# A two-layer gated cross-attention and expert kernel: another order of gathers, posts and sends, and idle products

## The reference

```
x = x + tanh(g_xattn[0]) * causal_attention(layernorm(x), ctx, ctx)       # 16 heads of 32
x = x + tanh(g_ffn[0])   * experts(layernorm(x))                          # 32 experts, 8 chosen per row
x = x + tanh(g_xattn[1]) * cross_attention(layernorm(x), ctx, weights)    # q, k, v projections, RMS norms, output projection
x = x + tanh(g_ffn[1])   * (layernorm(x) @ ternary(weight).T + bias)
```

## Time and profile before

| | |
|---|---|
| median of three runs | 1456.93 us |
| the profiled execution | 1449.55 us |
| its span, first to last instruction | 1447.8 us |
| TensorE busy | 1290.1 us (89%), mean granted clock 0.963 |
| VectorE, ScalarE, POOL busy | 940.0, 897.2, 519.5 us |
| gathers of rows (L709), 120 | 191.2 us of POOL |
| first layer | up to about 297 us |
| experts | about 297 to 922 us |
| second layer | from about 922 us |

### The profile page before, as it was taken

One profiled execution on the slowest core, in us unless ns is written; L12 is line 12 of the kernel. 1 busy time (PEld: TensorE's weight loads), 2 busy tenths in 40 slices (PEclk: granted clock), 3 DMA queues, 4 the chain that ended last, 5 costly groups with the idle time before them and its releaser, 6 DMA issues. The chain is left out here.

```text
span 1447.8 us, 39176 instructions
## 1 busy us (share of the span) xinstructions
PE 1290.1 (89%) x11501; PEld 836.5 (58%) x11502; DVE 940.0 (65%) x2347; ACT 897.2 (62%) x1845; POOL 519.5 (36%) x537
## 2 busy tenths in 40 slices
PE   3999999559999999999999999756899999999984
PEld 3777777425556656665556666333565656656652
DVE  4699897655566655656555633164777888888863
ACT  4777776325566666666566666425667777777661
POOL 2036564664335333321000000655544555552000
PEclk9999999779999999999999999978999999999997
DMA  3036445499888676766766544856646646653000
GB/s 104 31 130 224 181 171 184 173 311 324 290 309 282 235 234 226 244 213 215 233 229 210 193 146 145 167 89 88 102 69 108 106 71 117 103 72 75 16 8 23
DMA packets 96136, 233.49 MB, mean 161 GB/s; under 512 B 11808, under 2 KB 11808, under 8 KB 91424
## 3 DMA queue, kind: packets, MB, share of 16 engines
q0 software_dynamic: 33712, 113.79, 31.5%
q1 hardware_dynamic: 62320, 118.34, 24.6%
HBM read 140.84 MB, written 91.24 MB: 160 GB/s over the span
## 5 line engine op out<-in xcount | busy, mean ns | idle before, releaser
L1614 PE MATMUL bank<-wh,xT 128*128 x1280 | 340.1, 328 | 6.3 <-DVE hp L1729 5.4
L709 POOL DMA_INDIRECT xs<-y_tiles,slot_ix x120 | 191.2, 1593 | 219.9 <-DMA y_tiles<-ysb 99.9
L1614 PE MATMUL bank<-wl,xT 128*128 x640 | 209.4, 327 | 0.0
L1719 DVE SCALAR_TENSOR_TENSOR hv<-bank,sg 128x192 f32<-128x192 f32 x160 | 57.0, 356 | 220.1 <-ACT sg L1673 174.6
L1688 ACT ACTIVATE ysb<-bank,xg 128x512 f32<-128x512 f32 x160 | 110.0, 687 | 117.5 <-PE bank L1638 117.5
L1614 PEld LDWEIGHTS bank<-wh,xT 128*128 128x128 f16 x1280 | 125.6, 98 | 83.6 <-issue 13.4
L1667 ACT ACTIVATE xT<-bank 128x1024 f16<-128x1024 f16 x160 | 162.7, 1017 | 15.3 <-PE bank L1602 15.3
L1638 PE MATMUL bank<-wh,hT 128*128 x480 | 155.8, 379 | 0.8 <-issue 0.5
L1849 PE MATMUL bank<-w_hi,halfT 128*128 128x512 f16 x384 | 127.1, 393 | 23.5 <-DVE accb L1966 22.1
L334 ACT ACTIVATE l_probs<-bank,l_bias 128x256 f32<-128x256 f32 x256 | 118.9, 473 | 39.0 <-DVE l_bias L368 38.6
L1508 POOL DMA_DIRECT2D raw<-in_experts_dram x30 | 16.8, 560 | 333.2 <-DVE wl L1745 325.4
(11 more groups left out here) (282 smaller groups left out, 3060.4 us busy)
## 6 DMA issues: line engine op xcount, KB each, us to landing
xg<-x_slots SPq DMA_DIRECT2D x160, 272.0 KB, 2.8
y_tiles<-ysb SPq DMA_DIRECT2D x160, 256.0 KB, 2.7
raw<-in_experts_dram POOLq DMA_DIRECT2D x30, 1280.0 KB, 7.3
x_slots<-blank SPq DMA_DIRECT2D x33, 272.0 KB, 4.0
xs<-in_x_dram SPq DMA_DIRECT2D x8, 512.0 KB, 6.4
cbuf<-in_ctx_dram SPq DMA_DIRECT2D x8, 512.0 KB, 4.4
stage<-in_mats_dram POOLq DMA_DIRECT2D x4, 1024.0 KB, 6.4
room<-in_ctx_dram SPq DMA_DIRECT2D x8, 512.0 KB, 5.7
```

The costliest lines, as they stand in the source:

```text
L709: return nc.gpsimd.indirect_dma_start(to, None, self.y_tiles[0 : (MT + 1 - k) * P, :], ix, compute_op=ALU.add)
L1614: last = nc.tensor.matmul(bGU[t.place % 2][:, 0:GU], xT[:, t.place % 2, xo + c * P : xo + (c + 1) * P], wp[:, bass.ds(w, 1), c * GU : (c + ...
```

## The change

- Six instead of four of batch 0's gather turns are in the experts' block (`LAST_ADDS`).
- In the second layer's opening three of batch 1's gathers come before POOL's "P1"; on VectorE xc moves ahead of P2, and xn and sx ahead of P3; on ScalarE sx moves ahead of k0 and k1.
- A table `LAST1` replaces `SIDE1` in batch 7: batch 6's pieces come earlier, and the pieces with "=" are batch 7's own, with t = 0. The bank's order of use in that batch is `LAST_USES`.
- Ten of POOL's sends at the first layer's end lose their waits.
- TensorE gets products into bank 3 whose result nobody reads: 18 after the sum of the ternary weights, 2 after each of x0 and x1, 16 at the end of the block.

```diff
-LAST_ADDS = 4
+LAST_ADDS = 2
@@ BEGIN1
-    act=["sc", "T0", "T1", "P0", "P1", "k0", "k1", "sx", "T2", "T3", "P4", "P5", "k2", "k3"],
+    act=["sc", "T0", "T1", "P0", "P1", "sx", "k0", "k1", "T2", "T3", "P4", "P5", "k2", "k3"],
     pool=["P1", "xc", "P5"],
-    dve=["sc", "P0", "P1", "P2", "P3", "xc", "xn", "sx", "k0", "k1", "P4", ...
+    dve=["sc", "P0", "P1", "xc", "P2", "xn", "sx", "P3", "k0", "k1", "P4", ...
@@
+LAST1 = dict(
+    pe={0: ["a0"], 1: ["a1"], 2: ["<c0"], 3: ["c1"], 4: ["<d0"], 5: ["<d1"], 8: ["<g0", "g1"], 9: ["h0"], 10: ["h1"], 11: ["=a0"],
+        13: ["<=c0"], 14: ["=d0"]},
+    act={1: ["b0", "b1"], 2: ["c0"], 3: ["c1"], 7: ["f0", "f1"], 8: ["g0"], 9: ["g1"], 12: ["=b0"], 13: ["=c0"]},
+    pool={5: ["d1"]},
+    dve={0: ["a0", "a1"], 1: ["b0"], 2: ["<b1"], 4: ["d0"], 5: ["d1"], 6: ["e"], 7: ["f0", "f1"], 10: ["h0"], 11: ["h1"],
+         12: ["<=a0", "=b0"], 15: ["=d0"]})
@@ side1
-def side1(table, b, step, early, do_prep, do_post):
+def side1(eng, b, step, early, do_prep, do_post):
+    table = LAST1[eng] if b.n == B - 1 else SIDE1[eng]
...
+        if piece.startswith("="):
+            do_post(b, piece[1:])
@@ layer0, POOL
-            for n in (1, 2):
-                pool.wait_ge(xe_norm, QT * (B - 1) + n)
-                send_next()
-            for n in (1, 2):
-                pool.wait_ge(post_copied, 2 * (B - 1) + n)
-                send_next()
-            for n in (11, 12, 13, 14, 16, 18):
-                pool.wait_ge(dve_post, marks + n)
+            while sends[0] < SENDS * (B - 1):
                 send_next()
@@ layer0, TensorE
+            pe.wait_ge(at.probs_made, 2 * PAIRS * B)
+            def warm_up(n):
+                for _ in range(n):
+                    nc.tensor.matmul(bank[3][:, :], at.stack[:, 0, 0, 0, 0:P], at.stack[:, 0, 0, 0:2, :].rearrange("p h q -> p (h q)"),
+                                     start=True, stop=True)
             for piece in last_pieces("pe"):
                 pe_post0(pe, end, piece)
                 if piece == "o3":
...
+                    warm_up(18)
+                elif piece in ("x0", "x1"):
+                    warm_up(2)
...
             nc.tensor.matmul(bHT[1][:, 0:E], shared.ones[0:1, :], plan.moved16[:, :], start=True, stop=True).then_inc(plan.tab_ps, 1)
+            warm_up(16)
@@ layer1
         USES = ["a0", "a1", "c0", "c1", "d0", "d1", "g0", "g1", "h0", "h1"]
+        LAST_USES = ["a0", "c0", "d0", "a1", "c1", "d1", "g0", "g1", "h0", "h1"]
...
+                if is_last(b):
+                    dve.wait_ge(at.probs_made, STEPS * b.n + STEPS // 2 * (t + 1))
+                    chain.link(v.reciprocal(rsum[:, t, :], at.sums[:, b.par, t, :]))
+                elif t == 0:
                     dve.wait_ge(at.probs_made, STEPS * b.n + STEPS)
                     chain.link(v.reciprocal(rsum[:, :, :], at.sums[:, b.par, :, :]))
@@ layer1, POOL
-            before = {"P1": 0, "xc": 0, "P5": 6}
+            before = {"P1": 3, "xc": 0, "P5": 6}
```

More of the change, by code:

```diff
@@ L219, in side1 @@
         piece = word.lstrip("<")
-        if piece in ORDER_PREP1:
+        if piece.startswith("="):
+            do_post(b, piece[1:])
+        elif piece in ORDER_PREP1:
             if b.n + 1 < B:
@@ L227, in last_pieces1 @@
 def last_pieces1(eng):
-    return [piece for piece in ORDER_POST1 if any(piece == word.lstrip("<") for words in SIDE1[eng].values() for word in words)]
+    done = [word.lstrip("<=") for words in LAST1[eng].values() for word in words if "=" in word]
+    return [piece for piece in ORDER_POST1 if any(piece == word.lstrip("<") for words in SIDE1[eng].values() for word in words) and piece not in done]
 class Attention:
@@ L1834, in layer1, with is_last, uses_of, reads_of @@
         USES = ["a0", "a1", "c0", "c1", "d0", "d1", "g0", "g1", "h0", "h1"]
+        LAST_USES = ["a0", "c0", "d0", "a1", "c1", "d1", "g0", "g1", "h0", "h1"]
         COPIED = ["c0", "c1", "g0", "g1"]
-        READ = [u for u in USES if u not in COPIED]
+        def is_last(b):
+            return isinstance(b.n, int) and b.n == B - 1
+        def uses_of(b):
+            return LAST_USES if is_last(b) else USES
+        def reads_of(b):
+            return [u for u in uses_of(b) if u not in COPIED]
         def mine(b, t):
@@ L1986, in pe_post @@
                 return
-            k, t = USES.index(piece), int(piece[1])
-            before = USES[k - 1]
+            k, t = uses_of(b).index(piece), int(piece[1])
+            before = uses_of(b)[k - 1]
             if before in COPIED:
@@ L1992, in pe_post @@
             else:
-                pe.wait_ge(po_read, 6 * b.n + 1 + (READ.index(before) + 1 if k else 0))
+                pe.wait_ge(po_read, 6 * b.n + 1 + (reads_of(b).index(before) + 1 if k else 0))
             if piece[0] == "a":
@@ L2011, in act_post @@
             elif piece in COPIED:
-                act.wait_ge(po_ps, 10 * b.n + USES.index(piece) + 1)
+                act.wait_ge(po_ps, 10 * b.n + uses_of(b).index(piece) + 1)
                 nc.scalar.activation(aT[:, t, :], bPost[:, :].bitcast(F16), ACT.Copy).then_inc(po_copied, 1)
@@ L2040, in dve_post_ @@
             elif piece[0] == "d":
-                dve.wait_ge(po_ps, 10 * b.n + 5 + t)
+                dve.wait_ge(po_ps, 10 * b.n + uses_of(b).index(piece) + 1)
                 v.scalar_tensor_tensor(att[:, t, :], bPost[:, :], 1.0 / (SC_A * SC_W), vec[:, B_O, :], ALU.mult, ALU.add).then_inc(po_read, 1)
-                dve.wait_ge(po_read, 6 * b.n + 4 + t)
+                dve.wait_ge(po_read, 6 * b.n + reads_of(b).index(piece) + 2)
                 chain.link(v.scalar_tensor_tensor(mine(b, t), att[:, t, :], gates[:, 1:2], mine(b, t), ALU.mult, ALU.add))
@@ L2061, in dve_post_ @@
                 v.scalar_tensor_tensor(outb[:, t, :], outb[:, t, :], gates[:, 3:4], mine(b, t), ALU.mult, ALU.add).then_inc(out_ready, 1)
-                if t == QT - 1:
+                if t == QT - 1 and not is_last(b):
                     chain.end("post1")
@@ L2122, in body @@
                 for s in range(STEPS):
-                    side1(SIDE1["pool"], b, s, False, lambda b, piece: pool_prep(pool, b, piece), lambda b, piece: pool_post(pool, b, piece))
+                    side1("pool", b, s, False, lambda b, piece: pool_prep(pool, b, piece), lambda b, piece: pool_post(pool, b, piece))
                     if b.n + 2 < B:
@@ L2142, in body @@
                     at.act_step(act, b, s, more)
-                    side1(SIDE1["act"], b, s, False, lambda b, piece: act_prep(act, b, piece), lambda b, piece: act_post(act, b, piece))
+                    side1("act", b, s, False, lambda b, piece: act_prep(act, b, piece), lambda b, piece: act_post(act, b, piece))
             over_batches(lambda b: body(b, True), lambda b: body(b, True), lambda b: body(b, False))
@@ L2201, in body @@
                 for s in range(STEPS):
-                    at.pe_step(pe, b, s, more, before=b.n > 0, between=lambda: side1(SIDE1["pe"], b, s, True, do_prep, do_post))
-                    side1(SIDE1["pe"], b, s, False, do_prep, do_post)
+                    at.pe_step(pe, b, s, more, before=b.n > 0, between=lambda: side1("pe", b, s, True, do_prep, do_post))
+                    side1("pe", b, s, False, do_prep, do_post)
             over_batches(lambda b: body(b, True), lambda b: body(b, True), lambda b: body(b, False))
```

10 lines of the change are left out of this document (5 added, 5 removed).

## The result

The changed kernel takes **1443.48 us** (median of seven runs, 1436.25 to 1447.47), the kernel before 1456.93 (seven runs in all, 1450.17 to 1463.98): ratio 0.9912, 95% interval 0.9884 to 0.994, so 0.9% faster, 12.8 us (13.45 by the two medians). Timed again later beside the same kernel before it was 0.9934 (0.9906 to 0.9962). The forecast was 1438 in a range of 1429 to 1450. The profiled execution took 1443.48 us, its span is 1441.7, which is 6.1 less than the 1447.8 of before.

A forecast was written before the change was run, and what follows sets the result against it. Three loose seams (first layer's end, second layer's start, kernel's end), the longest second-layer wait being VectorE's for batch 1's gathers. 10.2 + 2.4 + 2.2 = 14.8 us off the profiled 1449.55 gives 1434.8, median about 1438, range 1429 to 1450.

The forecast's parts named there:

- Gathers and beginning: Second layer's start: earlier gathers and VectorE's new order shorten the wait for batch 1's rows; 10.2 us won.
- The opening: Second layer's block: waits for turn 3's last gather to land, so it opens 4.8 us later.
- P1's lateness: Second layer's start: P1's three POOL operations run about 1.5 us late behind the third early gather; costed at nothing.
- First layer's end: From the first layer's end into the experts: warmed clock and earlier opening; 2.4 us counted, bounds 3.1 and 1.6.
- The first 22 products: First layer's end: they keep TensorE's clock up for x0, x1 and the gate products; 2.6 us won.
- Do they hold the end?: First layer's block end: whether the last 16 products delay it; claimed sequencers run ahead, cost taken as nothing.
- The prediction's own sign of being wrong: First layer's end: the experts opening after 297 us would show the forecast wrong; 294.4 was forecast.
- Rival A: First layer's block end waits for queued work, experts open 3.9 us later; 6 won, 1447 us; chance 0.13.
- Last batch: Batch 7: first half of its post work moves into steps 11 to 15; steps 4.1 us longer, 2.2 won overall.
- rival B: Last batch's order gains nothing, steps lengthen as much as the tail shrinks; 11 to 12 won, 1442 us; chance 0.22.
- The work behind the power stays: Kernel's end: the work after the last power (at 1430.05 us before) is unchanged by the last batch's new order.
- B and C: Rivals: last batch's order gains nothing (0.22); unread products do not warm the clock, 12 won, 1441 us (0.08).

The follow-up runs named there:

- no_products: Changed kernel without any of the products that nobody reads (18, 2, 2 and 16); 0.9889 of the kernel before.
- two_early_gathers: Changed kernel without the last 16 products, with two of batch 1's gathers ahead of P1 on POOL, not three; 0.9885 of the kernel before.
- changed_again: The changed kernel itself, unaltered, run again as comparison for a later group; 0.9934 of the kernel before, median 1443.38 us.
- old_order_25: Changed kernel without the last 16 products, last batch in old order, unread products in its tail, 25 behind d1; 0.9904 of before, 1508.85 us against 1524.4.
- last_batch_as_before: Changed kernel with the last batch in the old order, all of batch 7's post work behind its attention; 0.9921 of the kernel before.
- old_order_kept_warm: Changed kernel without the last 16 products, last batch in old order, 43 unread products in its tail, 16 behind d1; 0.9849 of before, 1433.97 us.
- no_last16: Changed kernel without the 16 products at the end of the first layer's block; 0.9899 of the kernel before, 1508.5 against 1522.4 us.

## Why the prediction was right, and where it was not

**Gathers and beginning: right.** Forecast 10.2 won, measured 10.0 (B 125.1 to 115.1, in both executions of the changed kernel), about 9.5 by the means of the executions without and with this part (125.5 and 116.0). The way there too: xc's power was to come 2.3 us earlier beside the experts' end and came 2.4 earlier (24.5 behind the last result, 26.9 before). The last of the 13 remaining gathers was forecast at 978.1; with the experts' end moved by 4.2 that is 982.3, and it left at 983.15. The opening was forecast 4.8 later and was 2.6 later in the profiled execution (4.2 behind the last result, before 1.5). In all eleven executions with six turns it was 4.2 to 6.6 behind, 3.9 later on their mean. The length of B does not follow it (115.1 us in no_products, which opened 5.9 behind), since P0 and P1 are not what xc waits for. P1's lateness I had costed at nothing: it held x's normalising for 2.00 us, and two_early_gathers shows that taking this away brings nothing, so nothing is the right cost, for another reason than mine: the gathers behind it set the pace. VectorE's waits are 7.5 us and not about 4: VectorE reaches them earlier by what it won at the start.

**First layer's end: wrong by 5 us.** The first 22 products did their part (2.6 forecast, 2.4 by the stretches). (The 3.1 us from which the recorded text counts down to 2.4 is in none of its own terms, which give 2.6.) The step that failed is "Do they hold the end? ... sequencers run ahead, and the end is the sequencer's ... I take nothing". The end waits until the products are through: 0.38 us from the end of the last one to the table load (299.95, 300.33), 0.38 again in changed_again (294.61 + 6.01 = 300.62, 301.00). So 2.4 us won became about 3 lost: the stretch from the last copy of the attention's result to the table load is 28.9 us before, 31.3 and 32.5 changed. The prediction's own sign of being wrong, that the experts open after 297, came with it. My evidence was of another kind: TensorE's queue fetches the tile's code ahead of products in flight, and POOL's sequencer passes sends that its engine has not begun. Neither shows what the block's end asks of TensorE. What it asks is the DRAIN on TensorE's queue, 5.33 us in the changed kernel and 6.02 in changed_again. The trace of the kernel before had it, 0.26 us long, in the rows of the block's change (L786); the prediction does not use it. POOL's queue has none, and there the inference holds at the next change: the second layer opens at 928.97 while the last gather of the old block begins at 930.71. The sentence beside it, from the Trainium skill, page "TensorE: Matmul & The Clock Gate" (Architectural detail), that TensorE's queue holds 64, would have covered all 32 instructions; a queue's length was no answer to what the end waits for, and the trace decides against using it so. No run here shows the 64 itself.

Rival A had this mechanism at 0.13, with 6 us won in the profiled execution, and 6.1 is what the two profiles differ by. Its other half, that the opening of the second layer would eat 2 of the 10 us, did not come: B kept all 10.

**Last batch: the tail right, the steps wrong.** The tail was to shrink by 6.3 us and shrank by 5.7. The steps were to grow by 4.1 and grew by 6.3 on the mean, 5.6 between the two profiled executions. In those the term that was mis-sized is the stalls. TensorE's gaps in C were 6.4 us before (mostly 4.15 before g0) and are 8.8 in the changed kernel: g0 0.7, g1 0.8, h0 1.0, h1 0.7, a0 0.7, c0 0.7 and two of 1.6 and 1.9 elsewhere. I had each at 0.7 to 1.0, but took the sum for little more than what g0 gave back: 0.2 us (4.1 less the 3.9 of work), and it was 2.4. The work itself grew by 3.1 us there (59.1 to 62.3 busy), less than the 3.9 forecast.

On the mean a second thing comes in, which the prediction had at nothing: the clock of the steps. In three of the nine executions of the new order TensorE ran at clock 0.50 for some 6 to 10 us around g0 to h0, the steps whose gaps are listed above; the changed kernel's profiled execution is not one of them. changed_again (columns as in rows 1), 67.8 us busy in C:

```profile
1389.00:1398.50 9.50, 8.79 (x47) 4.99 (x46) 2.66 (x6) 5.29 (x14) 0.00 (x0) 0.50 0.01 2
```

So 2.2 won became 0.6 lost: rival B, at 0.22. "The work behind the power stays" is right on the mean; that E was 2 us longer in the profiled execution is the clock at h1, which is met at either level in either order.

**The sum.** By the stretches 10.0 - 3.0 - 0.6 = 6.4 us won against the 14.8 forecast, and 6.1 by the two spans; the timed medians say 13.45 and 12.4, the ratios 12.8 and 9.6. The profiled execution of before (1449.55 us) is below all seven of its timed runs and 7.4 under their median, so the spans understate the gain. Where an average execution of before loses the rest of it I cannot say: the experts' stretch alone, which the change does not touch, scatters from 620 to 628 us over the fourteen executions. The time came out in the range because one term carried the forecast and was right, while the two wrong ones cost 8 us, which the scatter of the executions hides in part. That the median stands only 5.5 us from the 1438 is to that extent luck. (The chances do not add up either: six tenths of 0.52 and half of B and C are 0.46 for more than 1%, not 0.54.) The better kernels follow from the same reading: the change without its last 16 products, with a filled tail.

## What to carry to other kernels

Work that nobody reads may fill a gap that ends with a wait of its own engine, but not the last place in front of a block's end: there it was waited for in full. The rows of the change from block to block name what it waits for on each queue, so read them before arguing from what a sequencer does elsewhere. Ahead of a chain of dependent gathers, moving links forward counts (three were worth 7 to 8 us here), and what was won on POOL beside the chain was lost again at its end. Work moved into full steps costs its own length plus each new hand-over, here six of 0.7 to 1.0 us, and in some executions the clock of the steps around them.

## What the runs showed of the hardware

- The change from one block to the next waited for TensorE's products to be through (0.36 to 0.38 us from the end of the last one to the next block's first instruction, in all seven executions with them; TensorE's DRAIN there took 5.0 to 6.0 us, and 0.26 in the seven without), but not for POOL's issued gathers (opened at 928.97, last gather begun at 930.71; no DRAIN on its queue in any of the fourteen traces).
- The granted clock differs between executions of one kernel. In the sparse tail h1 took 3.60 us in the changed kernel and 1.90 in changed_again, at 1.2 and at 2.4 GHz; in the last batch's steps (C) it was the other way, 1.00 and 0.91, 71.1 and 75.4 us. With 2 to 7 products in each short gap and 25 in the long one it was 0.97 of full speed from the attention's end to the end (old_order_25), and 0.70 and 0.72 in the same order without any (last_batch_as_before, before). With 16 in the long gap and 2.39 us of idle time behind them it was 0.92, and the second turn took 1.03 us and not 0.62 (old_order_kept_warm).
- Two chips differed by 4.6 to 4.7% on the same kernel (1455.8 and 1522.4 to 1524.4 us for the kernel before), and in the kernels profiled on the slower one nearly all of it lay in the first 335 us. Up to about 80 us the pace was the same (TensorE busy 18.9 us from 60 to 80 in the changed kernel and in no_last16); from 100 to 135 it was 33.0 against 27.5. Why, no run here shows.
